# Expert feed-forward in a two-layer decoder: features on partitions, the expert's weights copied first, orders shifted by a block

## What is computed

```python
logits = x @ gate_w.T + gate_b
topk_logits, topk_idx = jax.lax.top_k(logits, K)          # K = 4 of E = 32
topk_weight = jax.nn.softmax(topk_logits, axis=-1)
gate = ragged_dot(xt, w_gate, group_sizes) + b_gate[gid]   # [256 -> 128] for each expert
up = ragged_dot(xt, w_up, group_sizes) + b_up[gid]
gate = jnp.minimum(gate, 7.0)
up = jnp.clip(up, -7.0, 7.0)
activated = (up + 1.0) * gate * sigmoid(1.702 * gate)
outs = ragged_dot(activated, w_down, group_sizes) + b_down[gid]   # [128 -> 256]
y = jnp.sum(outs * topk_weight[..., None], axis=1)
```

## Time and profile before

| | us |
|---|---|
| median of 3 runs | 1018.72 |
| the profiled execution, its own time | 1018.88 |
| span of the trace of that execution | 1017.2 |
| TensorE busy over the span | 809.6 (80%) |
| VectorE busy | 749.9 (74%) |
| ScalarE busy | 488.3 (48%) |
| GpSimd busy | 459.5 (45%) |

### The profile page before, as it was taken

How to read it: one execution, slowest core, us unless ns; L and a number is a source line. 1 busy time by engine, 2 the same in 40 slices (tenths; PEclk the granted TensorE clock), 3 DMA queues, 4 the chain that set the end, 5 groups by cost and what they waited for, 6 DMA issues and landing times. The chain is left out here.

```text
span 1017.2 us, 16391 instructions
## 1 busy us (share of the span) xinstructions
PE 809.6 (80%) x4620; PEld 608.5 (60%) x4624; DVE 749.9 (74%) x1562; ACT 488.3 (48%) x1262; POOL 459.5 (45%) x512
## 2 busy tenths in 40 slices
PE   6798999999799999429999933577799999980165
PEld 3477999997699998317777721224455555550133
DVE  2576777777688887585666635787799999959977
ACT  0233444444355555003333312258898878608185
POOL 1004444442455553536555537140588889813111
PEclk9879999999999999558999975788799999995577
DMA  8707000000400001003444435100333323110000
GB/s 291 245 1 319 14 0 0 0 0 1 174 2 0 0 0 36 6 13 108 125 128 124 124 125 188 60 0 4 124 103 104 99 87 104 42 42 0 0 11 32
DMA packets 29836, 72.06 MB, mean 71 GB/s; under 512 B 5362, under 2 KB 19314, under 8 KB 27298
## 3 DMA queue, kind: packets, MB, share of 16 engines
q1 hardware_dynamic: 25186, 58.95, 16.6%
q0 software_dynamic: 4608, 12.59, 4.7%
HBM read 60.97 MB, written 10.55 MB: 70 GB/s over the span
## 5 line engine op out<-in xcount | busy, mean ns | idle before, releaser
L1718 POOL TENSOR_TENSOR arena<-arena 128x1024 f32<-128x1024 f32 x63 | 147.6, 2371 | 30.7 <-DVE arena L1684 30.7
L1684 DVE TENSOR_TENSOR_SCAN arena<-arena,ps 128x1024 f32<-128x1024 f32 x64 | 143.5, 2275 | 13.6 <-PE ps L1605 8.5
L662 POOL TENSOR_TENSOR arena<-arena 128x256 f32<-128x256 f32 x64 | 46.6, 728 | 195.4 <-DVE arena L656 195.4
L1625 PE MATMUL ps<-arena 128*128 128x512 f32 x256 | 120.1, 592 | 0.0
L712 ACT ACTIVATE arena<-arena 128x128 f32<-128x128 f32 x256 | 98.9, 390 | 19.3 <-DVE arena L682 18.7
L721 ACT ACTIVATE arena<-ps 128x512 f32<-128x512 f32 x64 | 38.2, 598 | 131.4 <-PE ps L609 131.4
L589 PE MATMUL ps<-arena 128*128 (+3 forms) x768 | 96.8, 277 | 2.5 <-PEq L731 0.9
L589 PEld LDWEIGHTS ps<-arena 128*128 128x128 f32 (+1 forms) x768 | 91.5, 193 | 4.1 <-issue 2.9
L1650 ACT ACTIVATE arena<-arena 128x1016 f32<-128x1016 f32 x64 | 72.4, 1135 | 22.9 <-DVE arena L1684 22.8
L1660 ACT ACTIVATE arena<-arena 128x256 f32<-128x256 f32 x192 | 81.2, 494 | 0.1
L1060 POOL DMA_INDIRECT arena<-tokens,arena x64 | 64.0, 1000 | 28.8 <-issue 23.4
(11 more groups left out here) (319 smaller groups left out, 1786.0 us busy)
## 6 DMA issues: line engine op xcount, KB each, us to landing
arena<-c_rows SPq DMA_DIRECT2D x32, 512.0 KB, 3.7
arena<-in_E_gu SPq DMA_DIRECT2D x8, 1024.0 KB, 12.1
expert_out<-arena SPq DMA_DIRECT2D x64, 128.0 KB
arena<-in_E_dn SPq DMA_DIRECT2D x1, 4096.0 KB, 13.7
arena<-in_ctxT SPq DMA_DIRECT2D x2, 1024.0 KB, 5.2
arena<-in_X_o SPq DMA_DIRECT2D x1, 2048.0 KB, 19.9
arena<-in_A_o SPq DMA_DIRECT2D x1, 2048.0 KB, 27.2
arena<-in_F_w SPq DMA_DIRECT2D x2, 1024.0 KB
```

Of the source, the lines that this page charges most:

```text
L1625: t = eng.matmul(ps[:, 2 * k + half, :], ident, hC[s % 4][:, half * 512:(half + 1) * 512], start=False, stop=n == ST - 1)
L1684: eng.tensor_tensor_scan(hst[s % 4], dA[s % 4], psD[s % 2].rearrange("p k m -> p (k m)"), 0.0, ALU.mult, ALU.add).then_inc(h_ready, 1)
L1718: eng.tensor_tensor(hC[s % 4], hst[s % 4], Csb[i % 4], ALU.mult).then_inc(hC_ready, 1)
```

## The change

Both the layout and the orders of the expert stage change. In short:
- **Layout.** The gate and up results now have features on partitions and tokens in the free dimension: the expert's weights are the stationary operand, and `xinT` streams (four matmuls of 128 columns for two of 256). The product can then go straight into the down matmul as its stationary operand, so `TA` and `AT` are gone.
- **Weight copy.** ScalarE first copies the expert's whole gate and up weights (128 x 512) from `wgu` to a double buffer `wcur` (`weights`), at an address from a register that it loads from `owner_i`.
- **Biases.** The gate and up biases are now one value for each partition, and go into the two limiting instructions of VectorE, which loads the expert's number into a register too. Both bias matmuls and `split3` are gone. The down bias is added in the combine stage: the softmax weights are spread to a token x expert table, which TensorE transposes and multiplies by the down biases, and VectorE adds that to `x`.
- **Orders.** Nothing is a loop now: all 64 blocks are written out. GpSimd no longer copies the token numbers. Per turn s, TensorE does turn(s+2), gate_up(s+1), down(s-1); ScalarE tokens(s+2), sigmoid(s+1), weights(s+2); VectorE limits(s+1), gated(s), rows(s-1).

Lines taken out are left out here, since the stage before is printed above; lines without a sign are kept from it.

```diff
+        bias_gu = view(A0 + 10240, 2 * E, "p (e k) -> p e k", k=2)
+        bias_dn = view(A0 + 10304, D)
+        weightT = view(A0 + 10560, 256, "p (g t) -> p g t", g=2)
...
+            load(eng, "bias", bias_gu, a["E_bias"])
+            load(eng, "bias_dn", bias_dn, a["E_bias_dn"])
...
             @block.gpsimd
...
+        wcur = view(o, 1024, "p (d c m) -> p d c m", d=2, c=DC); o += 1024
...
+        spread = view(o, 256, "p (b e) -> p b e", b=NB); o += 256
+        assert o <= 51104
...
         with nc.Block() as block:
             @block.gpsimd
             def _(eng):
+                for s in range(NBLK):
+                    u = s % 4
+                    if s >= 4:
                         eng.wait_ge(xT_done, s - 3)
                     eng.indirect_dma_start(xin[:, u], None, hd,
+                                           bass.IndirectOffsetOnAxis(ap=tok_i[:, s:s + 1].bitcast(u32), axis=0)
                                            ).then_inc(x_in[u], 16)
             @block.sync
             def _(eng):
+                for s in range(NBLK):
+                    u = s % 4
                     eng.wait_ge(y_ready, s + 1)
+                    eng.dma_start(ys[s * P:(s + 1) * P, :], yout[:, u]).then_inc(y_out[u], 16)
                 for u in range(4):
                     eng.wait_ge(y_out[u], 16 * (NBLK // 4))
             @block.tensor
             def _(eng):
+                def turn(s):
+                    d, u = s % 2, s % 4
+                    eng.wait_ge(x_in[u], 16 * (s // 4) + 16)
+                    if s >= 2:
                         eng.wait_ge(xT_ready, s - 1)
                     for c in range(DC):
                         t = eng.transpose(ps[:, d, c * P:(c + 1) * P], xin[:, u, c * P:(c + 1) * P], ident)
                     t.then_inc(xT_done, 1)
+                def gate_up(s):
+                    d = s % 2
                     eng.wait_ge(xT_ready, s + 1)
+                    eng.wait_ge(w_ready, s + 1)
+                    if s >= 2:
                         eng.wait_ge(up_ready, s - 1)
+                    for k in range(2):
+                        for c in range(DC):
+                            t = eng.matmul(ps[:, 2 + d, k * I:(k + 1) * I], wcur[:, d, c, k * I:(k + 1) * I],
+                                           xinT[:, d, c, :], start=c == 0, stop=c == DC - 1)
+                    t.then_inc(gu_done, 1)
+                e_next, e_down = eng.alloc_register("e_next"), eng.alloc_register("e_down")
+                def down(s):
+                    d = s % 2
+                    e = eng.snap(e_down, min_val=0, max_val=E - 1)
                     eng.wait_ge(act_ready, s + 1)
+                    if s >= 2:
                         eng.wait_ge(y_ready, s - 1)
+                    eng.matmul(ps[:, 6 + d, 0:D], act_[:, d], wdn[:, bass.ds(e, 1), :].rearrange("p a m -> p (a m)"),
+                               start=True, stop=True).then_inc(dn_done, 1)
+                loaded(eng, "wgu", "wdn")
+                eng.reg_load(e_next, owner_i[0:1, 0:1])
+                eng.wait_ge(spread_step, 2)
+                for g in range(2):
+                    t = eng.transpose(ps[:, 4, g * P:(g + 1) * P],
+                                      spread[:, 4 * g:4 * g + 4].rearrange("p b e -> p (b e)"), ident)
+                t.then_inc(wT_done, 1)
+                turn(0)
+                turn(1)
+                gate_up(0)
+                for s in range(NBLK + 1):
+                    if s + 2 < NBLK:
+                        turn(s + 2)
+                    if s + 1 < NBLK:
+                        gate_up(s + 1)
+                    if s >= 1:
+                        down(s - 1)
+                    if s < NBLK:
+                        eng.reg_mov(e_down, e_next)
+                    if s + 1 < NBLK:
+                        eng.reg_load(e_next, owner_i[0:1, s + 1:s + 2])
             @block.scalar
             def _(eng):
+                def tokens(s):
+                    d = s % 2
                     eng.wait_ge(xT_done, s + 1)
+                    if s >= 2:
                         eng.wait_ge(gu_done, s - 1)
                     eng.activation(xinT[:, d], ps[:, d, 0:D].rearrange("p (c t) -> p c t", c=DC),
                                    ACT.Copy).then_inc(xT_ready, 1)
+                def sigmoid(s):
+                    d = s % 2
                     eng.wait_ge(gate_ready, s + 1)
+                    if s >= 2:
                         eng.wait_ge(gs_ready, s - 1)
                     eng.activation(sig[:, d], gate[:, d], ACT.Sigmoid, scale=1.702).then_inc(sig_ready, 1)
+                e_a = eng.alloc_register("e_a")
+                def weights(s):
+                    eng.reg_load(e_a, owner_i[0:1, s:s + 1])
+                    if s >= 2:
+                        eng.wait_ge(gu_done, s - 1)
+                    e = eng.snap(e_a, min_val=0, max_val=E - 1)
+                    eng.activation(wcur[:, s % 2], wgu[:, :, bass.ds(e, 1), :].rearrange("p c a m -> p c (a m)"),
+                                   ACT.Copy).then_inc(w_ready, 1)
+                loaded(eng, "wgu")
+                weights(0)
+                eng.wait_ge(wT_done, 1)
+                eng.activation(weightT, ps[:, 4, 0:2 * P].rearrange("p (g t) -> p g t", g=2), ACT.Copy).then_inc(wT_ready, 1)
+                tokens(0)
+                weights(1)
+                tokens(1)
+                sigmoid(0)
+                for s in range(NBLK):
+                    if s + 2 < NBLK:
+                        tokens(s + 2)
+                    if s + 1 < NBLK:
+                        sigmoid(s + 1)
+                    if s + 2 < NBLK:
+                        weights(s + 2)
             @block.vector
             def _(eng):
+                e_w = eng.alloc_register("e_w")
+                def rows(s):
+                    u = s % 4
+                    eng.wait_ge(dn_done, s + 1)
+                    if s >= 4:
+                        eng.wait_ge(y_out[u], 16 * (s // 4))
+                    eng.tensor_copy(yout[:, u], ps[:, 6 + s % 2, 0:D]).then_inc(y_ready, 1)
+                def limits(s):
+                    d = s % 2
+                    eng.reg_load(e_w, owner_i[0:1, s:s + 1])
+                    e = eng.snap(e_w, min_val=0, max_val=E - 1)
                     eng.wait_ge(gu_done, s + 1)
+                    if s >= 2:
+                        eng.wait_ge(act_ready, s - 1)
+                    eng.tensor_scalar(gate[:, d], ps[:, 2 + d, 0:I], bias_gu[:, bass.ds(e, 1), 0], 7.0, ALU.add,
+                                      ALU.min).then_inc(gate_ready, 1)
+                    eng.tensor_scalar(up[:, d], ps[:, 2 + d, I:2 * I], bias_gu[:, bass.ds(e, 1), 1], 8.0, ALU.add,
+                                      ALU.min).then_inc(up_ready, 1)
+                def gated(s):
+                    d = s % 2
                     eng.wait_ge(sig_ready, s + 1)
                     eng.tensor_tensor(gate[:, d], gate[:, d], sig[:, d], ALU.mult).then_inc(gs_ready, 1)
                     eng.wait_ge(gs_ready, s + 1)
+                    if s >= 2:
+                        eng.wait_ge(dn_done, s - 1)
                     eng.scalar_tensor_tensor(act_[:, d], up[:, d], -6.0, gate[:, d], ALU.max,
                                              ALU.mult).then_inc(act_ready, 1)
+                loaded(eng, "wgu", "bias")
+                eng.tensor_scalar(bias_gu[:, :, 1], bias_gu[:, :, 1], 1.0, None, ALU.add).then_inc(bias_step, 1)
+                eng.tensor_tensor(prod, pick, gw.rearrange("p b k -> p (b k)").unsqueeze(2).to_broadcast([P, NB * TOPK, E]),
+                                  ALU.mult).then_inc(spread_step, 1)
+                eng.wait_ge(spread_step, 1)
+                eng.tensor_reduce(spread, prod.rearrange("p (b k) e -> p b e k", b=NB), AX.X, ALU.add).then_inc(spread_step, 1)
+                eng.wait_ge(bias_step, 1)
+                limits(0)
+                for s in range(NBLK + 1):
+                    if s + 1 < NBLK:
+                        limits(s + 1)
+                    if s < NBLK:
+                        gated(s)
+                    if s >= 1:
+                        rows(s - 1)
         first_layer.close()
...
+        s_comb, bias_done = sem("combine_step"), sem("down_bias_done")
...
             @block.tensor
...
+                for b in range(NB):
+                    rows = slice((b % 4) * E, (b % 4 + 1) * E)
+                    t = eng.matmul(ps[:, b, 0:D], weightT[rows, b // 4], bias_dn[rows],
+                                   start=True, stop=True)
+                    if b % 2:
+                        t.then_inc(bias_done, 1)
...
+                for k in range(NB // 2):
+                    eng.wait_ge(bias_done, k + 1)
+                    two = x[:, 2 * k:2 * k + 2]
+                    ch.mark(eng.tensor_tensor(two, two, ps[:, 2 * k:2 * k + 2, 0:D], ALU.add))
+                ch.wait()
...
```

(66 more changed lines are left out.)

67 lines of the change are left out of this document (6 added, 61 removed).

## The result

The changed kernel takes 1065.8 us (median of 4 runs, 1062.01 to 1069.73) against 1019.8 (4 runs, 1017.98 to 1022.2): a ratio of 1.045, 95% interval 1.0404 to 1.0496. The forecast was 1054, with a range of 1034 to 1083. The profiled execution of the changed kernel took 1069.73 us, span 1068.0, and is the longest of the four.

The account below looks back on a forecast made before the run. TensorE bounds the expert stage before (2.078 us a block); afterwards a closed loop through TensorE, VectorE and ScalarE takes 2.65. The stage's end shifts from 595.2 to 630.3, so 1018.9 + 35.1 = 1054 us, range 1034 to 1083.

Parts of the forecast that it names:

- The closed circle through three engines: Expert stage: each gate_up waits for weights copy, behind sigmoid, behind limit, behind the previous gate_up; 2.65 us a block.
- The sum of the block: Expert stage, one block: 1.20 + 0.32 + 0.45 + 0.63 + 0.05 = 2.65 us, low 2.35, high 2.99.
- Loads of gate_up start to VectorE's first read: TensorE to VectorE in a block: eight float32 entries of 128 columns behind a wait, 1.20 us.
- A pointer operand in place of a constant: VectorE's limit of gate: reading the bias by pointer instead of a constant adds nothing.
- limit to sigmoid: VectorE's limit of gate to ScalarE's sigmoid in a block: 0.32 us.
- sigmoid to copy: ScalarE, sigmoid's start to weights copy's start: register load plus 0.15 for issue and address, 0.45 us.
- rival 2: ScalarE's register load is slow or waits for a drain: block 2.95 us or more, 1073 us and up; chance 0.06.
- Rival 1: Expert stage: TensorE's clock falls as it streams only 58%; 1110 us, or 1082 for half the time; chance 0.11.
- rival 3: Expert stage: loop does not close, VectorE's 1.8 to 1.9 us sets the pace; 1007.5 us; chance 0.05.
- Start: Expert stage's beginning: limit of block 1 at 461.6 us, plus 1.8 for two blocks at half clock.
- End: Expert stage's end: block 63's limit at 627.7, then 2.6 us to the last copy of rows, 630.3.
- Combine: Combine stage: eight bias matmuls, 6.9 us, and four additions of 0.69 hide in waits; adds nothing.

Follow-up runs that it names:

- copy-first: Changed kernel with ScalarE's weights(s+2) ahead of sigmoid(s+1), nothing else changed; 999.25 us, ratio 0.9785 to the kernel before.
- all loads early: Against copy-first: TensorE's, ScalarE's and VectorE's register loads each issued behind an instruction that covers them; 1002.12 us, ratio 0.983 to the kernel before.

## Why the prediction was right, and what its sum left out

- **The closed circle through three engines** is the cause. The exchange of two calls takes it away with 66.6 us, the third buffer leaves it, and four edits of its links shorten the block by what they take from the link.
- **The sum of the block** was 0.18 us short, 2.65 against 2.83, and that is 62 x 0.18 = 11.2 us. In the profiled execution the stage became 46.4 us longer where 35.1 were foreseen, 11.3 more. (The forecast also lies 11.8 below the median of 1065.8. That the two figures agree so well is luck: the traced execution is 3.9 above the median, and 4.5 of its us lie outside the stage.) The mechanism was right and two terms were mis-sized. "Loads of gate_up start to VectorE's first read", taken as 1.20, measured 1.32: the neighbouring rows had readers with fixed addresses, and I had counted VectorE's register load ahead of the wait but not the arithmetic behind it. "A pointer operand in place of a constant I cost at nothing" was 0.06 us, and limit to sigmoid 0.39 for 0.32. The other terms: 0.45 for sigmoid to copy measured 0.42 (the load beside the sigmoid plus 0.15, as it was reasoned), 0.63 for the copy measured 0.63, 0.05 measured 0.07.
- **The register load** on ScalarE takes 0.278 us (median) and not longer, so rival 2 falls. The figure of about 600 ns from the Trainium skill, "DMA: Bandwidth & Descriptors", section "Latency and other measured facts", doesn't hold for this load: 278 ns on ScalarE and 304 on VectorE here, as 304 on TensorE. In copy-first, from 480 to 560 us, ScalarE's load has a median of 490 ns, and single ones take up to 659.
- **The clock** stays at 1.00 with TensorE busy 50.38 of 80 us and idle for about 1 us in each block. Rival 1 falls: the swing between the two levels that it was built on does not occur here.
- **Faster** (rival 3) needed the copy ahead of the sigmoid. That order gives 999.25, and its price was put at 1007.5: the block falls to 1.72, where I had put 1.8 to 1.9.
- **Start.** Block 1's limit was put at 461.6 and came at 464.12, of which 2.1 us lie ahead of the stage. 1.8 us more for the clock's rise were about 1 us too many: from there to the last limit it is 176.3 us where 166.1 were foreseen, and 62 x 0.18 would make it 177.3.
- **End.** Last limit to last copy of rows: 643.70 - 640.4 = 3.3 us, put at 2.6.
- **Combine.** From the first gather to the first combination 6.57 us, before 6.51: hidden, as foreseen. The 6.9 us of bias matmuls in that working were far too many; they took 2.09. (Its end, "about 606.9", should also read 607.1 by its own terms, 599.5 + 6.9 + 0.69; nothing hangs on it.)
- **The loop's removal "covered"**: in the changed kernel nothing shows it, but without the circle it is worth 12.6 us (1019.64 - 1007.05). In the rival's price I gave it nothing.

## What to carry to other kernels

When an engine's written order puts work for block s+2 behind work for block s+1, ask whether the first feeds the engine that the second waits for: if so, the order is a circle, its length is the sum of one pass, another buffer does not shorten it (here a third one left 2.84 us), and exchanging two calls may be worth more than the change itself. Price such a circle link by link, and count behind each wait also the register arithmetic of an instruction whose address comes from a register. Compare a change that also writes out a loop with the old kernel written out, or the loop's price is booked to the wrong part.

## What the runs showed of the hardware that was not expected

- An address from a register costs VectorE 0.12 us behind a wait (1.32 against 1.20 from loads to limit; the row FUSED_REGOPS has 69 ns of it), even with the load ahead of the wait. A pointer operand makes a 128x128 TENSOR_SCALAR 351 ns long instead of 292.
- A register load from SBUF has no fixed length: medians of 278 ns (ScalarE, changed kernel), 304 (VectorE, the same), 490 (ScalarE, copy-first) and 493 (VectorE, all loads early), the last two from 480 to 560 us.
- The hardware loop around the stages of the kernel before costs 0.18 us a block of 2.08.
- Sixteen float32 entries of 32 rows and 256 columns (eight matmuls) took 2.09 us in a stretch (646 to 650 us) with a granted clock of 0.50, the lower level. Four entries of 128 rows and 256 columns took 1.95 us at that level. The entries of 32 rows use different groups of rows in turn and may run beside each other; that is not shown, since no run tried them in one group.
- Idle time of TensorE's weight loads named "issue" (9.9 us in 80, in front of L1067) can be removed whole without the block getting shorter. It overlaps matmuls: TensorE is busy 79.83 of 80 us beside it.
